# Cross-attention with operands as pairs: from f32r pairs in two passes over head groups to fp16 pairs with scales in one pass per batch

## The reference

```python
Q = (x @ Wq + bq).reshape(b, s, H, DH).transpose(0, 2, 1, 3)
K = (c @ Wk + bk).reshape(b, s, H, DH).transpose(0, 2, 1, 3)
V = (c @ Wv + bv).reshape(b, s, H, DH).transpose(0, 2, 1, 3)
scores = einsum('bhqd,bhkd->bhqk', Q, K) / sqrt(DH) * mask
attn = softmax(scores)
out = einsum('bhqk,bhkd->bhqd', attn, V).transpose(0, 2, 1, 3).reshape(b, s, H * DH) @ Wo + bo
y = x + out; return layernorm(y) * gamma + beta
```

## Time and profile before

| | us |
|---|---|
| three runs: median (lowest to highest) | 2381.5 (2380.4 to 2382.26) |
| the profiled execution, its own time | 2381.32 |
| its span, first to last instruction | 2379.5 |
| TensorE busy | 2299.0 (97%) |
| VectorE busy | 1983.5 (83%) |
| ScalarE busy | 1789.5 (75%) |
| GpSimd busy | 1263.9 (53%) |

### The profile page before, as it was taken

One profiled execution on the slowest core, in us unless ns is written; L12 is line 12 of the kernel. 1 busy time (PEld: TensorE's weight loads), 2 busy tenths in 40 slices (PEclk: granted clock), 3 DMA queues, 4 the chain that ended last, 5 costly groups with the idle time before them and its releaser, 6 DMA issues.

```text
span 2379.5 us, 47987 instructions
## 1 busy us (share of the span) xinstructions
PE 2299.0 (97%) x12352; PEld 1565.4 (66%) x12352; DVE 1983.5 (83%) x4296; ACT 1789.5 (75%) x3809; POOL 1263.9 (53%) x1704
## 2 busy tenths in 40 slices
PE   5899999999999999999899999999999999999994
PEld 4566666666666666666566666666666666666662
DVE  5788888888788888788787989988989988999883
ACT  4777777777777777777677877788887778777773
POOL 2454444555444555444443666565666665666645
PEclk9999999999999999999999999999999999999997
DMA  3978878777878787877879888778778777777764
GB/s 129 195 174 195 203 184 191 189 194 185 206 188 191 183 198 181 206 190 190 200 183 203 189 190 198 192 187 198 191 187 192 195 188 196 188 189 193 197 158 115
DMA packets 1165324, 446.02 MB, mean 187 GB/s; under 512 B 1078880, under 2 KB 1078880, under 8 KB 1165280
## 3 DMA queue, kind: packets, MB, share of 16 engines
q1 hardware_dynamic: 1161728, 444.70, 77.6%
q10 hardware_dynamic: 3552, 0.80, 0.2%
HBM read 143.41 MB, written 33.55 MB: 74 GB/s over the span
## 4 chain that ended last, share of the span: by engine, by line
PE 93%; DVE 2%; DMA 2%; POOL 1%; ACT 1%; issue 1%; SPq 0%; POOLq 0%; DVEq 0%
PE fill_ps L340 22%; PE fill_ps L341 19%; PE fill_ps L342 19%; PE ctx_ps L423 14%; PE score_ps L388 8%; PE score_ps L391 5%; PE score_ps L394 5%; DMA pT<-p 1%; DVE score_ps L709 1%; DMA raw<-in_ct 0%; DVE p L725 0%; SPq L232 0%; POOL acc L1039 0%; POOL acc L1041 0%; ACT probs L526 0%
## 5 line engine op out<-in xcount | busy, mean ns | idle before, releaser
L709 DVE CUSTOM_DVE_ANT_0 score_ps<-score_ps,mask_sb 128x512 f32<-128x512 f32 x1024 | 693.4, 705 | 279.8 <-PE score_ps L394 272.0
L526 ACT ACTIVATE probs<-score_ps,neg_max 128x512 f32<-128x512 f32 x1024 | 696.6, 684 | 300.1 <-POOL neg_max L976 297.8
L725 DVE SCALAR_TENSOR_TENSOR p<-probs,inv_sum,p 128x512 f16<-128x512 f32 x896 | 750.9, 857 | 49.6 <-ACT p L539 49.6
L539 ACT ACTIVATE p<-probs,inv_sum 128x512 f16<-128x512 f32 x1024 | 706.6, 718 | 29.9 <-DVE inv_sum L718 24.9
L976 POOL TENSOR_SCALAR neg_max<-row_max 128x2 f32<-128x2 f32 x512 | 173.2, 338 | 628.2 <-DVE row_max L709 622.0
L423 PE MATMUL ctx_ps<-pT,v 128*64 128x512 f16 x3072 | 364.9, 388 | 16.4 <-DMA pT<-p 8.5
L423 PEld LDWEIGHTS ctx_ps<-pT,v 128*64 128x64 f16 x3072 | 168.3, 111 | 198.4 <-issue 72.5
L388 PE MATMUL score_ps<-k_hi,q_hi 64*128 64x512 f32 x1024 | 250.9, 477 | 17.0 <-ACT probs L526 15.3
L340 PE MATMUL fill_ps<-xT_hi,wq_hi 128*128 128x512 f32 x512 | 216.1, 422 | 24.1 <-DVE wq_lo L699 24.0
L340 PE MATMUL fill_ps<-cT_hi,wk_hi 128*128 128x512 f32 x512 | 210.7, 412 | 3.4 <-POOL cT_lo L968 2.2
L340 PE MATMUL fill_ps<-wo_hi,ctx_hi 128*128 128x512 f32 x512 | 211.9, 414 | 0.8 <-DVE acc L799 0.8
(11 more groups left out here) (71 smaller groups left out, 4226.6 us busy)
## 6 DMA issues: line engine op xcount, KB each, us to landing
raw<-in_xt SPq DMA_DIRECT2D x128, 256.0 KB, 3.1
raw<-in_ct SPq DMA_DIRECT2D x128, 256.0 KB, 3.3
mask_sb<-in_mask_Bx1xSxS_fk SPq DMA_DIRECT2D x128, 256.0 KB, 2.9
acc<-in_x SPq DMA_DIRECT2D x64, 256.0 KB, 2.9
partial<-acc SPq DMA_DIRECT2D x64, 256.0 KB, 2.4
acc<-partial SPq DMA_DIRECT2D x64, 256.0 KB, 2.8
out<-acc SPq DMA_DIRECT2D x64, 256.0 KB, 2.1
pT<-p SPq DMA_TRANSPOSE x512, 3.8
```

The costliest lines, as they stand in the source:

```text
L526: nc.scalar.activation(probs[:, i % E_TILES, :], score_ps[:, i % 4, :], ACT.Exp, bias=neg_max[:, p % 2, i:i + 1], accum_out=row_sum[:, p % ...
L539: nc.scalar.activation(p16[:, q, a, 0, :], probs[:, i % E_TILES, :], ACT.Copy, scale=inv_sum[:, p % 2, i:i + 1]).then_inc(p_rounded, 1)
L709: nc.vector.tensor_tensor_reduce(out=score_ps[:, i % 4, :], in0=score_ps[:, i % 4, :], in1=mask_sb[:, q, :], scale=SCORE_SCALE, scalar=-3. ...
L725: nc.vector.scalar_tensor_tensor(out=p16[:, q, a, 1, :], in0=probs[:, i % E_TILES, :], scalar=inv_sum[:, p % 2, i:i + 1], in1=p16[:, q, a, ...
```

## The change

All f32r pairs become fp16 pairs. To keep fp16 in range, scales are formed on the chip:

- Each weight matrix gets one scale from its row maxima: VectorE takes maxima (`weight_maxima`), a matmul with a matrix of ones sums them over partitions, and three small VectorE instructions make the scale (`weight_scale`). ScalarE rounds the scaled weight (`round_weight`), VectorE makes the rest (`split_weight`).
- For each batch VectorE takes maxima of x and c (eight tiles per batch; before, the four tiles of c in either pass), three products with bounds of the weights, one matmul over three columns, and two small instructions give the scales of x, c and V (`bound_products`, `bound_inputs`, `input_scale`). The scores are multiplied back inside the mask instruction, and the output blocks in the addition to `acc`. GpSimd scales the biases of Q and K (`scale_biases`).
- bv is no longer added to the attention output. Once, at the start, eight f32 matmuls form bv times Wo (`bias_output`), and VectorE adds it to bo. The first `values` block waits for that (`bo_ready`).

Both weight halves lie in SBUF at once, so there is one pass: 16 repetitions of eight pairs. The projections Q, K and V have eight blocks each per batch, and the four output blocks have 24 matmuls each. The DRAM buffer `partial` is gone; x is loaded into `acc`, and out stored, once per batch. The weights are loaded whole (2 MB each) at the start, into places that probabilities and attention output use later, and are split there.

The inputs are rounded by ScalarE (`round_input`), both x and c. The fp16 pairs of x and c have one place each, so the rounding of x waits for the last Q block of the batch, and that of c for its last K and V blocks. GpSimd then scales the raw tile in place and subtracts (`split_input`, two instructions per tile). GpSimd no longer splits any probability tile (`POOL_TILES = ()`), VectorE does all eight. V has one place of four blocks, so V4 to V7 are evacuated after `values` of pair 3.

SP's list keeps four transposes per pair, issues the loads of x and c early in the body, and those of the mask between the transposes of pair 6. The core of the diff:

```diff
-POOL_TILES = (7,)
+POOL_TILES = ()
...
+        w16 = {w: sb(f"w{w}16", [P, DT, 2, WIDTH], F16) for w in "qkv"}
+        w16["o"] = sb("wo16", [P, PAIRS, 2, D], F16)
+        xc16 = {t: sb(f"{t}T16", [P, DT, 2, S], F16) for t in "xc"}
+        qk16 = {t: sb(f"{t}16", [P, 2, 2, S], F16) for t in "qk"}
+        v16 = sb("v16", [P, 1, KT, 2, GW], F16)
...
+        def weight_tile(w, j):
+            if w == "o":
+                return staged["o"][:, j, :], w16["o"][:, j, 0, :], w16["o"][:, j, 1, :]
+            cut = slice(j // DT * GW, (j // DT + 1) * GW)
+            return staged[w][:, j % DT, cut], w16[w][:, j % DT, 0, cut], w16[w][:, j % DT, 1, cut]
 
         def batches(eng, body):
-            body(None, None, (0, 0, 0), None, 0)
-            for g in range(GROUPS):
-                body(*around(g, 0, True, False), g, None)
-                with eng.Fori(1, B - 1) as b:
-                    body(*around(g, b, False, False), None, None)
-                body(*around(g, B - 1, False, True), None, g + 1 if g + 1 < GROUPS else None)
-            body((GROUPS - 1, B - 1, LAST), None, None, None, None)
+            body(None, None, 0, False)
+            body(None, 0, 1, True)
+            with eng.Fori(1, B - 1) as b:
+                body(b - 1, b, b + 1, False)
+            body(B - 2, B - 1, None, False)
+            body(B - 1, None, None, False)
 
         def wait_alone(eng, semaphore, value):
             eng.wait_ge(semaphore, value)
...
+            def start():
+                load_input(0, "x", range(DT), early=True)
+                load_weight("q")
+                load_input(0, "c", range(DT), early=True)
+                load_weight("k")
+                load_mask(0, range(QT), early=True)
+                load_weight("v")
+                for dst, vec in ((bo_b, bo), (gamma_b, gamma), (beta_b, beta)):
+                    sp.dma_start(dst[:, :], vec.partition_broadcast(P)).then_inc(rows_in, DMA)
+                load_weight("o")
...
+            def bias_output():
+                pe.wait_ge(vo_back_ready, 1)
+                pe.wait_ge(scale_ready, 3)
+                pe.wait_ge(bias_in, 3 * DMA)
+                for j in range(PAIRS):
+                    mm = nc.tensor.matmul(ctx_ps[:, :], bias_col["v"][:, j:j + 1].to_broadcast([P, P]), staged["o"][:, j, :],
+                                          start=j == 0, stop=j == PAIRS - 1)
+                mm.then_inc(bias_out_ready, 1)
...
-                        lhs, rhs = (w_hi[w][:, part, cols], w_lo[w][:, part, cols]), (xc_hi[t][:, part, :], xc_lo[t][:, part, :])
+                            pe.wait_ge(xc_split[t], n * DT + j + 1)
+                        cut = slice(k * P, (k + 1) * P)
+                        lhs, rhs = [w16[w][:, j, l, cut] for l in (0, 1)], [xc16[t][:, j, l, :] for l in (0, 1)]
...
+                    for lq, lk in ((0, 0), (1, 0), (0, 1)):
+                        for a in range(2):
+                            if lq == lk:
+                                free = tile_no(n, p, 2 * q + a) - 4
+                                if not (isinstance(free, int) and free <= 0):
+                                    pe.wait_ge(exp_done, free)
+                            mm = nc.tensor.matmul(banks[a], qk16["q"][halves[a], par, lq, cut],
+                                                  qk16["k"][halves[a], par, lk, :], start=lq == lk, stop=lk == 1)
+                            if lk == 1:
+                                mm.then_inc(s_ready, 1)
...
+                    scores(here, 6, range(0, 1))
+                    fill(here, "V", 6)
+                    fill(here, "Q", 7)
+                    scores(here, 6, range(1, 2))
+                    fill(here, "K", 7)
+                    fill(here, "V", 7)
+                    scores(here, 6, range(2, 4))
+                    values(here, 4)
+                    scores(here, 7, range(0, 1))
+                if opening:
+                    sum_weight_rows("v")
+                    sum_first_bound(2)
+                if nxt is not None:
+                    fill(nxt, "K", 0)
+                if here is not None:
+                    scores(here, 7, range(1, 2))
+                if nxt is not None:
                     fill(nxt, "Q", 0)
-                if here:
-                    scores(here, 3, range(2, 3))
-                if nxt:
+                if here is not None:
+                    scores(here, 7, range(2, 3))
+                if nxt is not None:
+                    fill(nxt, "K", 1)
+                if here is not None:
+                    scores(here, 7, range(3, 4))
+                    values(here, 5)
+                if nxt is not None:
+                    scores(nxt, 0, range(0, 1))
                     fill(nxt, "Q", 1)
-                    fill(nxt, "K", 0)
...
+            def round_input(n, t, tiles, early=False):
+                if is_first(n) and not early:
+                    return
+                c = "xc".index(t)
                 for i in tiles:
+                    if i == 0:
+                        act.wait_ge(scale_ready, c + 1 if is_first(n) else bound_no(n))
+                        if not is_first(n):
+                            act.wait_ge(qk_ready["QK"[c]], n * PAIRS)
+                            if t == "c":
+                                act.wait_ge(v_ready, n * 2 * KT)
+                    nc.scalar.activation(xc16[t][:, i, 0, :], raw_input(t, i), ACT.Copy,
+                                         scale=scale[:, c:c + 1]).then_inc(xc_rounded[t], 1)
...
+                    round_probs(here, 5, range(3, 6))
+                if nxt is not None:
+                    round_input(nxt, "x", range(0, 2))
+                if here is not None:
+                    exponentials(here, 6, range(0, 2))
+                if nxt is not None:
+                    round_input(nxt, "x", range(2, 3))
+                if here is not None:
+                    round_probs(here, 5, range(6, 8))
+                    round_context(here, 3)
+                    exponentials(here, 6, range(2, 3))
+                if nxt is not None:
+                    round_input(nxt, "c", range(0, 1))
+                if here is not None:
+                    evacuate(here, "Q", 7)
+                    exponentials(here, 6, range(3, 4))
+                if nxt is not None:
+                    round_input(nxt, "c", range(1, 2))
+                if here is not None:
+                    evacuate(here, "V", 7)
+                if nxt is not None:
+                    round_input(nxt, "c", range(2, 3))
+                if here is not None:
+                    evacuate(here, "K", 7)
+                    round_probs(here, 6, range(0, 1))
+                if nxt is not None:
+                    round_input(nxt, "c", range(3, 4))
+                if here is not None:
+                    exponentials(here, 6, range(4, 6))
+                    round_probs(here, 6, range(1, 2))
+                if nxt is not None:
+                    round_input(nxt, "x", range(3, 4))
...
+            def split_weight(w):
+                for j in range(PAIRS):
+                    dve.wait_ge(w_rounded[w], j + 1)
+                    src, hi, lo = weight_tile(w, j)
+                    nc.vector.scalar_tensor_tensor(out=lo, in0=src, scalar=w_scale[w], in1=hi, op0=ALU.mult,
+                                                   op1=ALU.subtract).then_inc(w_split[w], 1)
...
-            def split_input(at, t, tiles):
-                g, b, n = at
+            def split_input(n, t, tiles):
+                c = "xc".index(t)
                 for i in tiles:
-                    if t == "c":
-                        wait_alone(pool, c_max_taken, n * DT + i + 1)
-                    if t == "x":
-                        wait_alone(pool, xc_in[i], (n + 1) * DMA)
-                        nc.gpsimd.tensor_scalar(xc_hi["x"][:, i, :], raw_input("x", i), 1.0, 1.0, ALU.mult,
-                                                ALU.mult).then_inc(x_rounded, 1)
-                    pool.wait_ge(x_rounded if t == "x" else c_rounded, n * DT + i + 1)
-                    nc.gpsimd.tensor_tensor(xc_lo[t][:, i, :], raw_input(t, i), xc_hi[t][:, i, :],
+                    wait_alone(pool, xc_rounded[t], n * DT + i + 1)
+                    wait_alone(pool, xc_max_taken[t], n * DT + i + 1)
+                    nc.gpsimd.tensor_scalar(raw_input(t, i), raw_input(t, i), scale[:, c:c + 1], 1.0, ALU.mult,
+                                            ALU.mult).then_inc(xc_scaled[t], 1)
+                    wait_alone(pool, xc_scaled[t], n * DT + i + 1)
+                    nc.gpsimd.tensor_tensor(xc16[t][:, i, 1, :], raw_input(t, i), xc16[t][:, i, 0, :],
                                             ALU.subtract).then_inc(xc_split[t], 1)
...
+                    negate_max(here, 6, range(0, 1))
+                if nxt is not None:
+                    split_input(nxt, "x", range(0, 2))
+                if here is not None:
```

(14 more changed lines are left out.)

## The result

The changed kernel takes 2449.3 us (median of 4 runs, 2445.9 to 2452.3) against 2381.0 before: 1.029 times the time, 95% interval 1.027 to 1.031. It is slower, and outside the range of the forecast (2298, 2220 to 2350). Its profiled execution took 2451.2 beside a span of 2449.4.

A forecast was written before the change was run, and what follows sets the result against it. The prediction took TensorE, busy for 97% of the span, as the bound. Start 118, first batch 118, 14 periods of 137.3 and tail 138 made 2296, plus 1.8 around the span: forecast 2298 us, range 2220 to 2350.

The forecast's parts named there:

- steady work: TensorE's matmuls per batch: 576 slots of 0.2175 us plus extras at block changes, 132.1 us in all against 142.3 before.
- handover: New fp16 inputs, Q7's end to K0: GpSimd's seven tiles make a 17.7 us chain, TensorE loses 3.6; all waits 5.2.
- The change part by part: The prediction's cost list for TensorE, VectorE, ScalarE, DMA, new waits, start, first batch and tail, summing to 2296 us.
- rival 3: At the handover GpSimd and VectorE block each other: chain 9.2 us longer, period 146.5, time 2427; chance 0.07.
- extra of a first matmul: In the 48 blocks per batch that are no V blocks, the first matmul costs 0.02 us more, 1.0 in all.
- Rival 4: In TensorE's blocks, fp16 does nothing for the projection pitch: 480 slots stay at 0.23 us, time 2420; chance 0.04.
- S71: Score block of pair 7's second query: waits for exponentials, as pair 6's last maxima stand behind c tile 3; 1.1 us.
- First batch: The first batch's period, without output blocks: 137.3 - 21 = 116 us on TensorE, bound by VectorE near 118.
- Start: Everything before the first V block, with all weights scaled and split at once: 118 us (105 to 135) against 83.4.
- tail: From V block 0 of the last batch to the end, with output blocks and norm: 138 us.
- VectorE and ScalarE: Work of these two engines per batch: VectorE 125.0 us (122.3 before), ScalarE unchanged at 110.6.
- Rival 2: VectorE is the bound: TensorE waits for exponentials in the dense part, period 141 us, time 2350; chance 0.21.

The follow-up runs named there:

- e1: The changed kernel with its loop of 14 middle batches written out as straight code: 2347.1 us, 0.986 times the kernel before.
- e2: The kernel before with two repetitions in each turn of its loops: 2415.0 us, ratio 1.016 to the kernel before.
- e11: The kernel before as straight code, without loops: 2380.7 us, ratio 1.000 to the kernel before.
- e3: The changed kernel, loop kept, with GpSimd scaling the raw x and c early, amid pairs 5 and 6: 2471.8 us, 1.039 times the kernel before.
- e7: The changed kernel as straight code, with GpSimd's small instructions of pairs 5 and 6 moved to ScalarE: 2373.8 us, 0.997 times the kernel before.
- e10: The changed kernel as straight code, only ScalarE's order changed (Q7, V7 evacuations and an exponential before c roundings): 2367.8 us, 0.995 times the kernel before.
- e6: The changed kernel, loop kept, with a constant instead of the per-batch score scale in VectorE's mask instruction: 2446.7 us.
- e9: The changed kernel as straight code, with small instructions of pairs 5 and 6 on ScalarE, early input scaling and ScalarE's new order: 2303.6 us, ratio 0.967.
- e5: The changed kernel as straight code with early scaling of the raw inputs, small instructions still on GpSimd: 2373.2 us, 0.997 times the kernel before.
- e4: The kernel before with f32r operands as fp16 pairs in own buffers, without scales of x, c and weights, V scaled to at most 2: 2227.5 us, ratio 0.9365.
- e12: The changed kernel with two batches in each turn of its loop: 2415.9 us, 1.015 times the kernel before.

## Why the prediction was wrong

The span by the prediction's terms: 122.6 + 138.4 + 13 x 147.2 + 140.4 + 134.4 = 2449.4 (the period of 140.4 has no jump in it), against 118 + 118 + 14 x 137.3 + 138 = 2296.2 forecast. The gap of 153.2 us splits so (the steady work is counted within the handover's net):

- **The loop with the long body, 103 us (13 x 7.9). This step was missing.** "The change part by part" costed engines, queues and waits, and put the jump back of a loop body twice as long at nothing, without saying so. e1 takes the cost away, e2 puts one of its kind into the kernel before, e11 shows that straight code doesn't pay it. Of each 7.9, 6.8 are the turn itself. What the engines wait for is "issue"; that this is the code's fetch is inferred from the instruction transfers at the turn and from body length, and was not measured by itself. The label alone proves little: e1 has fifteen waits of ScalarE for "issue" before a Q evacuation, 1.5 each, where the changed kernel's profile puts fourteen of 1.6 down to GpSimd's scaled biases. None of the rivals held it: rival 3 gave 2427 for the slower side, by another mechanism. The Trainium skill would have told me where to look: by "Runtime: NRT & Kernel Launch" (Instruction fetch mechanics), code is fetched ahead only straight on, and a taken branch to code outside the current window must be fetched before the engine goes on. The traces agree (e1, e2 and e11 above), and add the price. The page's window, 512 instructions for most engines and 2048 for TensorE, no run here shows.
- **The steady work, better than forecast.** Projection blocks take 2.60, and 2.69 behind a change of kind; e1's 139.2 less its excess of 8.6 is 130.6, against 132.1. The extra of a first matmul, which I took as 0.02, is 0.01 (0.23 for the first slot behind a change of kind, 0.22 for the others), near the nothing that the prediction drew from the Trainium skill ("TensorE: Matmul & The Clock Gate", Weight-path perf modes). The trace agrees with the page's fast load of such weights: these 128-column fp16 loads take 97 to 102 ns, where the earlier trace rows had 189 for f32r. Rival 4 is out.
- **The handover, mis-sized: 8.6 instead of 5.2, less the 1.5 of the steady work: net 2.0 per batch (139.3 against 137.3), 28 us.** (The last period adds 1, the 1.2 that looped periods without a jump have.) The 8.6 are e1's: 7.8 from the two score blocks to the end of V block 4, 0.8 in pair 7's score blocks. The place was right (from V7 on) and the mechanism half so. The step said that K0 would wait for GpSimd's seven tiles; K0 hardly waits. Small instructions on GpSimd wait behind those tiles, and TensorE stops at the two score blocks and V block 4 before it ever reaches K0. I had that wait for one query, S71, with 1.1; it decides already at pair 6 (e3, e7, e10). And I had no term for the clock: of the 8.6, 2.6 are V block 4 running at half clock behind the stall (5.26 instead of 2.71 in e1).
- **First batch, 20 us.** "Without output blocks, 137.3 - 21" was a misreading: from V block 0 to the next, O2 and O3 of a batch before are missing, while O0 and O1 of batch 0 itself are there, so 10.5 and not 21, and 127 and not 118 by the prediction's own terms. Of the 11.6 left, some 3 are what the last period has too (140.4 against 137.3). The rest fits the stretch behind the first V block: from 125.9 to 138.3 TensorE stands 5.8 in five waits, the longest 1.96 for ScalarE's exponentials and one of 1.61 for K's split, and the granted clock is 0.88 from 122.6 to 150.
- **Start 122.6 against 118, tail 134.4 against 138.** The start is within its bounds of 105 to 135, the tail had none. bv times Wo took 9.7 where I took 7, and a wait of 5.7 for K's split before 119.94 stands in the start.
- **VectorE and ScalarE, right:** 124.3 and 110.3. For VectorE there is luck in it: the mask instruction's scale cost 3.3 per batch that I hadn't counted (64 x 0.052), and the 64 splits took 0.772 each in place of the 52.2 us that I had for them, 2.8 less. Rival 2 (VectorE's total) is refuted by e6 for the kernel as it is, though e9 shows its order to be what is late once the other two queues are repaired.
- **Rival 3.** I argued that both engines lose less than a whole instruction, which was too mild: e7's tiny products last as long as GpSimd's instruction beside them. This bears out the page "SBUF — State Buffer" of the Trainium skill (Who interferes with whom). In the changed kernel itself this was not what made it slower: GpSimd's tiles took 0.91 + 0.18 + 1.31 for x in the mean, in sum between the two ends of the earlier trace rows, and in the handover shown its longest tile took 2.97, under the 3 us that I had named as rival 3's sign.

## What to carry to other kernels

When loop bodies are merged, look whether instruction transfers now lie inside the loops of the trace and whether engines wait for "issue" once per turn: here that cost 6.8 us at each jump back on a batch of 147, and straight code, one line away, saved 7.9. An in-order engine that serves others with tiny results must not have large work queued ahead of them; price each handover by what stands behind it in the queue, on all engines together, since repairs on one of them alone made it worse three times (e3 or e5, e7, e10). And test the operand format by itself first: e4, without the scales, gained 6.35%.

## What the runs showed of the hardware that I had not expected

- A jump back cost 6.8 us with a body of one batch, 9.4 with two batches (e12), 2.8 in the mean with two old repetitions (e2), and nothing that shows with one (e11). The engines don't pay alike: in e2 VectorE's longest wait was 3.7, TensorE's 2.5. In the changed kernel TensorE has no such wait, in e12 one of up to 2.5 at each jump.
- Two VectorE instructions on 128 x 4 elements took 1.04 and 1.27 us beside a GpSimd instruction on 128 x 512, ending within 0.02 us of it, and 0.22 or less without (e7, e1).
- Behind TensorE's stalls the granted clock was near 0.5 (1.2 of 2.4 GHz) for some microseconds: 0.51 over the eight slots behind the 5.13 at the loop's turn, 0.57 over V block 4 behind waits of 1.73, 1.47 and 0.97. The mean clock went from 0.989 to 0.958 in the changed kernel and is 0.979 in e9.
- A per-partition scale from SBUF in the mask instruction costs 50 ns of 754 (e6).
